# The head and the tail of a conditioned two-layer kernel: earlier weight transfers, one more table pair before the first layer, and GpSimd's store ahead of its power

## The chip, the core and the metric

The kernel runs on one core of a Trainium2 chip. The core has five engines with a queue each: TensorE (PE in the rows, PEld for its weight loads), VectorE (DVE), ScalarE (ACT), GpSimd (POOL) and SyncE (SP), which only issues transfers. ACT and POOL issue transfers too. The metric is the device time of one execution in microseconds; the median of three is quoted. The profile is one further execution; its span runs from the first to the last recorded instruction.

## What is computed

128 sequences of 64 tokens with 256 features go through two layers. The first is chosen for each sequence by `itok_B_0_2` (kind NR, TSR or SR, else nothing is added), the second by one of 16 experts (`itok_B_0_15`). Both end in a residual and a layer norm.

```
out_nr  = gelu(x @ w1_nr + b1_nr) @ w2_nr + b2_nr
out_tsr = gelu(x @ w1_tsr + b1_tsr) @ w2_tsr + b2_tsr
out_sr  = gelu(gelu(x @ w1_sr + b1_sr) @ w2_sr + b2_sr) @ w3_sr + b3_sr
out = where(c == 0, out_nr, where(c == 1, out_tsr, where(c == 2, out_sr, 0)))
x = layernorm(x + out) * gamma + beta
...
hidden = gelu(x @ down_W.T + down_b)
hidden = hidden @ expert_W[idx].T + expert_b[idx]        # if the domain is valid
hidden = (hidden + domain_emb[idx]) @ up_W.T + up_b
return layernorm(hidden + x) * ln_gamma + ln_beta
```

## The kernel before

**Sort.** A head sorts the sequences by kind on the core itself: VectorE makes one-hot columns of the ids, TensorE sums them up, VectorE turns the sums into a place for each sequence. The result is `MOVES`, rows to load and to store (semaphores `s_load_ids`, `s_store_ids`), and `IDS`. From then on the work goes in slots of four sequences of one kind, 256 tokens each; with padding there are 33 slots here, 0 to 32.

**Precision.** Every operand of a large product is split in a high and a low part: ACT copies the high part (`weight_high`, `table_high`, `input_high`), VectorE subtracts it from the full value (`weight_low`, `table_low`, `input_low`), GpSimd does so for the hidden values (`low`). TensorE multiplies high by high, high by low and low by high.

**Tables.** The expert's matrix and the up projection are folded into one table for each expert. `table_pair(j)` makes two of 18 tables on TensorE, `table_high(j)` and `table_low(j)` split them. The pairs use three banks of PSUM in turn (`table_bank`), so from the fourth on (j = 3) a pair waits until the low part of an earlier one is taken. In the kernel before, three pairs (`EARLY_PAIRS`) are made in the head; pairs 3 and 4 come in step -1, 5 and 6 in step 0, 7 and 8 in step 1 (`PAIRS_IN_STEP`).

**Steps.** Every engine runs its own stream of steps, written out by hand in a fixed order: step g holds the layers of slot g and g + 1 and the later stages of slots g - 1 to g - 4. Steps -1 to 3 are unrolled (HEAD); then come a loop of plain steps (MAIN), a loop whose steps look at the number of slots (LATE), and DRAIN, the two steps behind the last slot. In step -1 TensorE runs the first layer of slot 0 (`start_sr`, 24 products), the tables of the step and the residual of slot 0, which waits for `s_store_ids`. In step 0 it runs half of the middle layer (`middle_layer`, with `w2_sr`), then the first half of slot 1's first layer, which waits for `x_lo`, the low part of slot 1's input.

**Queues in the head.** SP issues ids, `w1_sr`, `w1_two`, and once the sort is done two sequences of slot 0 and four of slot 1. ACT issues the first part of `per_unit` and of `per_feature` and the last bias, copies the high part of `w1_sr`, waits for the sort, issues the other two sequences of slot 0 and then `w2_sr`, the rest of `per_unit`, `last` and the rest of `per_feature`. Only then does it take up the tables and the input.

**Stores.** A slot's output goes out in two ways: SP stores one half with plain transfers, GpSimd the other with an indirect one (`store_tile`, 128 rows of 1 KB). VectorE's `finish` writes the output buffer of a slot and waits first for three things: `rstd` (the power that GpSimd computes), and for both stores of the slot before that used this buffer (`st_out`, `sc_out`). There are two buffers, so slot 30 waits for slot 28. In the last LATE step (g = 32) GpSimd computes power 32, then power 33, then stores slot 28. In DRAIN it stores 29 and 30 and computes power 34, then computes power 35 and stores 31 and 32.

The rows of the profile leave out numbers in names: `w_sr_sb` is w1_sr or w2_sr, `w_two` is w1_two, `x` is the input of either parity.

## Time and profile before

| | us |
|---|---|
| median of 3 runs | 293.97 |
| lowest, highest | 293.71, 295.15 |
| profiled execution, own time | 294.8 |
| profiled execution, span | 293.0 |
| TensorE busy in the span | 267.2 |
| VectorE, ScalarE, GpSimd busy | 197.2, 203.5, 149.4 |

The own time of the profiled execution is 1.8 us above its span: what lies around the recorded instructions. It is 0.83 us above the median. TensorE is busy nearly without a gap from 25 us to 258 us; it has idle time in the head, while the sort runs and the first weights and inputs come in, and in the tail, from 263 us on. After 286 us only transfers and the end of the program are left.

### The profile page before, as it was taken

How to read it: one execution, taken by the hardware profiler on the slowest of the kernel's cores; microseconds unless marked ns; L12 is line 12 of the kernel's file. 1: busy time of each engine (PE TensorE's matmuls, PEld its weight loads, DVE VectorE, ACT ScalarE, POOL GpSimd, SP SyncE). 2: the span in 40 equal slices, each digit the busy share in tenths (PEclk: the TensorE clock that was granted, in tenths of full speed). 3: DMA queues.
4: the chain of work that ended last, by engine and by line, in shares of the span. 5: the costliest groups of instructions: out<-in, count | busy, mean ns of one | idle time of the engine just before them, and what ended most of it. 6: DMA issues, size and time to landing. Idle time of an engine off the chain costs nothing.

```text
span 293.0 us, 8411 instructions
## 1 busy us (share of the span) xinstructions
PE 267.2 (91%) x2053; PEld 255.3 (87%) x2054; DVE 197.2 (67%) x669; ACT 203.5 (69%) x451; POOL 149.4 (51%) x164
## 2 busy tenths in 40 slices
PE   6879999999999999899999999999999999998410
PEld 6669999999999998799999999999999999997310
DVE  7486623426744844778888788888788887878360
ACT  3157687867777683887878888878878788776100
POOL 3211724734746654556655566545656455562450
PEclk9997999999999999999999999999999999999955
DMA  6561210110221122123242332423223332311121
GB/s 200 138 198 26 57 36 2 41 39 10 47 72 37 49 59 55 35 72 81 71 111 78 88 81 69 101 81 98 73 70 101 86 99 72 92 38 45 57 66 36
DMA packets 44029, 21.00 MB, mean 72 GB/s; under 512 B 37783, under 2 KB 42182, under 8 KB 44008
## 3 DMA queue, kind: packets, MB, share of 16 engines
q1 hardware_dynamic: 41142, 13.95, 19.7%
q0 software_dynamic: 1584, 4.33, 4.1%
q10 hardware_dynamic: 1282, 2.45, 2.8%
q8 instruction: 11, 0.18, 0.3%
q14 instruction: 10, 0.08, 0.1%
HBM read 12.02 MB, written 8.65 MB: 71 GB/s over the span
## 4 chain that ended last, share of the span: by engine, by line
PE 80%; issue 7%; DMA 4%; DVE 3%; POOL 2%; ACT 1%; ACTq 1%; POOLq 1%; DVEq 0%
PE ps_h L943 18%; PE ps_z L1012 10%; PE ps_u L1058 9%; PE ps_d L1067 9%; PE ps_z L1017 5%; PE ps_z L978 5%; PE ps_t L1029 5%; PE ps_u L978 4%; PE ps_t L1116 3%; PE ps_t L1117 3%; PE ps_z L1000 3%; PE ps_t L1119 3%; DMA w_sr_sb<-in_w_sr 2%; DMA out<-o,out_rows_now 1%; PE ps_u L912 1%
## 5 line engine op out<-in xcount | busy, mean ns | idle before, releaser
L446 POOL TENSOR_TENSOR h_lo<-h,h_hi 128x256 fp32r<-128x256 f32 (+1 forms) x75 | 69.7, 930 | 95.6 <-ACT h L805 95.5
L451 POOL TENSOR_TENSOR rs<-ve,minus_half 128x4 f32<-128x4 f32 x36 | 40.9, 1135 | 26.7 <-DVE ve L642 26.6
L805 ACT ACTIVATE h_hi<-ps_h,per_feature_sb 128x256 fp32r<-128x256 f32 x84 | 38.2, 479 | 20.3 <-PE ps_h L943 20.1
L630 DVE BATCH_NORM_STATS2 st<-ps_z 128x6 f32<-128x256 f32 x66 | 24.8, 414 | 33.1 <-PE ps_z L1017 33.1
L812 ACT ACTIVATE zn<-ps_z,nm,rs 128x256 f32<-128x256 f32 x66 | 33.7, 561 | 9.1 <-DVE nm L646 8.5
L461 POOL DMA_INDIRECT out<-o,out_rows_now x33 | 34.9, 1057 | 9.3 <-issue 6.1
L805 ACT ACTIVATE h<-ps_h,per_feature_sb 128x256 f32<-128x256 f32 x84 | 38.0, 481 | 0.0
L829 ACT ACTIVATE yt<-ps_t,per_feature_sb 128x256 f32<-128x256 f32 x66 | 34.0, 573 | 5.2 <-PE ps_t L1029 5.1
L1058 PE MATMUL ps_u<-table_hi,stack 128*128 x132 | 36.5, 306 | 0.0
L1067 PE MATMUL ps_d<-yt,per_feature_sb 128*128 128x256 f32 x132 | 34.1, 380 | 1.3 <-ACT yt L829 1.3
L1058 PE MATMUL ps_u<-table_lo,stack_hi 66*128 x132 | 33.7, 285 | 0.0
L602 DVE TENSOR_TENSOR x_lo<-x,x_hi 128x512 fp32r<-128x512 f32 x33 | 22.8, 690 | 14.9 <-ACT x_hi L787 14.9
L1012 PE MATMUL ps_z<-last_lo,h_hi 128*128 (+1 forms) x132 | 32.4, 279 | 0.0
L1012 PE MATMUL ps_z<-last_hi,h_hi 128*128 (+1 forms) x132 | 32.4, 279 | 0.0
L691 DVE SCALAR_TENSOR_TENSOR o<-n,rs,per_feature_sb 128x256 f32<-128x256 f32 x66 | 28.8, 477 | 0.0
L666 DVE SCALAR_TENSOR_TENSOR n<-ps_u,mv,per_feature_sb 128x256 f32<-128x256 f32 x66 | 28.2, 465 | 0.1
L943 PE MATMUL ps_h<-x_hi,w_two_lo 128*128 128x256 f32 x96 | 26.9, 280 | 0.0
L943 PE MATMUL ps_h<-x_hi,w_two_hi 128*128 128x256 f32 x96 | 26.9, 280 | 0.0
L943 PE MATMUL ps_h<-x_lo,w_two_hi 128*128 128x256 f32 x96 | 26.9, 280 | 0.0
L653 DVE BATCH_NORM_STATS2 st<-ps_u 128x6 f32<-128x256 f32 x66 | 25.0, 420 | 1.6 <-PE ps_u L1058 1.6
L1012 PEld LDWEIGHTS ps_z<-last_hi,h_hi 128*128 128x128 f32 x132 | 24.8, 188 | 1.1
L1012 PEld LDWEIGHTS ps_z<-last_lo,h_hi 128*128 128x128 f32 x132 | 24.8, 188 | 1.0
(153 smaller groups left out, 694.8 us busy)
## 6 DMA issues: line engine op xcount, KB each, us to landing
x<-in_x_feat SPq DMA_DIRECT2D x130, 64.0 KB
out<-o SPq DMA_DIRECT2D x66, 64.0 KB, 2.0
last_sb<-in_last_w ACTq DMA_DIRECT2D x1, 768.0 KB, 8.7
out<-o,out_rows_now POOLq DMA_INDIRECT x33, 2.7
w_sr_sb<-in_w_sr SPq DMA_DIRECT2D x1, 512.0 KB, 3.5
w_two_sb<-in_w_two SPq DMA_DIRECT2D x1, 512.0 KB, 4.3
w_sr_sb<-in_w_sr ACTq DMA_DIRECT2D x1, 512.0 KB, 6.6
per_unit_sb<-in_per_unit ACTq DMA_DIRECT2D x1, 325.0 KB
```

The lines of the kernel that those rows point to most:

```text
L446: pool.tensor_tensor(dst, full, high.bitcast(F32), ALU.subtract).then_inc(ready, 1)
L451: pool.tensor_tensor(RS[p][:, :, :], VE[p][:, :, :], mhalf[:, :].rearrange("p (n t) -> p n t", n=2), ALU.pow).then_inc(rstd, 1)
L461: pool.indirect_dma_start(out_rows, row, O[p][:, 1, :], None).then_inc(sc_out[p], 16)
L666: ins = dve.scalar_tensor_tensor(out=N2[p][:, t, :], in0=UP[p][:, t, :], scalar=MV[step][:, 1, t, 0:1], in1=G2[:, 0, :], op0=ALU.subtract, ...
L691: dve.scalar_tensor_tensor(out=O[q][:, t, :], in0=N2[q][:, t, :], scalar=RS[p][:, 1, t:t + 1], in1=G2[:, 1, :], op0=ALU.mult, op1=ALU.add) ...
L805: ins = act.activation(dst[:, m, :], src[m], ACT.Gelu, bias=COL[:, bass.ds(col + m, 1)])
L812: ins = act.activation(ZN[:, t, :], ZP[p][:, t, :], ACT.Identity, bias=NM[p][:, t:t + 1], scale=RS[p][:, 0, t:t + 1])
L829: ins = act.activation(YT[q][:, c, :], TP[:, c, :], ACT.Identity, bias=COL[:, COL_BETA1 + c:COL_BETA1 + c + 1], scale=COL[:, COL_G1 + c:CO ...
L943: ins = pe.matmul(out_ap, lhs[a], rhs[b], start=first and n == 0, stop=last and n == 2)
L1012: pe.matmul(ZP[p][:, t, :], h2h[:, c, t * P:(t + 1) * P], rows(half, c), start=False, stop=False)
L1058: ins = pe.matmul(UP[p][:, t, :], flat(stack[:, t, :, :])[:, d * T:d * T + P], table[:, bass.ds(at[2 * t + d], H)], start=False, stop=(tab ...
L1067: ins = pe.matmul(DP[:, 0:N], DD[:, c, :], YT[q][:, c, :], start=(c == 0), stop=(c == KC - 1))
```

## The change

In the head, ACT issues `w2_sr` and the rest of `per_unit` right behind its first two transfers, during the sort. `last` and the rest of `per_feature` go to SP, behind the input of slot 1. ACT warms up its gelu table ahead of all this, and copies the high part of `w1_two` during the sort instead of in step -1. Four table pairs are made in the head instead of three; ACT and VectorE take the first two ahead of the input of slot 0 (one before). The fourth stands on TensorE where six filler products (`keep_busy`) stood. Step -1 keeps pair 4 only. In a LATE step GpSimd stores before it computes the power of the step behind the last.

```diff
-        EARLY_PAIRS = 3
+        EARLY_PAIRS = 4
-        PAIRS_IN_STEP = {-1: (3, 4), 0: (5, 6), 1: (7, 8)}
+        PAIRS_IN_STEP = {-1: (4,), 0: (5, 6), 1: (7, 8)}
...
             load(rows_to_load(1), 1)
+            sp.dma_start(W["last"][:, :], W_DRAM["last"]).then_inc(s_w_in["last"], 16)
+            sp.dma_start(FEAT[:, EARLY_FEAT:], per_feature[:, EARLY_FEAT:]).then_inc(s_norm_in, 16)
...
+                store(g, p, where)
                 if where == LATE:
 
                     with pool.If(g + 1 >= n_slots):
                         power(g + 1, 1 - p)
-                store(g, p, where)
...
-            table_low(0)
+            for j in range(2):
+                table_low(j)
             input_low(0, 0)
...
-            for j in range(1, EARLY_PAIRS):
+            for j in range(2, EARLY_PAIRS):
                 table_low(j)
             weight_low("w2_sr")
...
+            act.wait_ge(s_const, 1)
+            act.activation(gelu_warm[:, :], ones[:, 0:1], ACT.Gelu)
             act.wait_ge(s_ids_in, 16)
             act.dma_start(UNIT[:, 0:EARLY_UNIT], per_unit[:, 0:EARLY_UNIT]).then_inc(s_unit_in, 16)
             act.dma_start(FEAT[:, 0:EARLY_FEAT], per_feature[:, 0:EARLY_FEAT]).then_inc(s_feat_in, 16)
+            act.dma_start(W["w2_sr"][:, :], W_DRAM["w2_sr"]).then_inc(s_w_in["w2_sr"], 16)
+            act.dma_start(UNIT[:, EARLY_UNIT:per_unit.shape[1]], per_unit[:, EARLY_UNIT:]).then_inc(s_unit_rest_in, 16)
...
-            act.wait_ge(s_const, 1)
-            act.activation(gelu_warm[:, :], ones[:, 0:1], ACT.Gelu)
             weight_high("w1_sr")
+            weight_high("w1_two")
...
-            act.dma_start(W["w2_sr"][:, :], W_DRAM["w2_sr"]).then_inc(s_w_in["w2_sr"], 16)
-            act.dma_start(UNIT[:, EARLY_UNIT:per_unit.shape[1]], per_unit[:, EARLY_UNIT:]).then_inc(s_unit_rest_in, 16)
-            act.dma_start(W["last"][:, :], W_DRAM["last"]).then_inc(s_w_in["last"], 16)
-            act.dma_start(FEAT[:, EARLY_FEAT:], per_feature[:, EARLY_FEAT:]).then_inc(s_norm_in, 16)
...
-            table_high(0)
+            for j in range(2):
+                table_high(j)
             input_high(0, 0, 0)
-            for j in range(1, EARLY_PAIRS):
+            for j in range(2, EARLY_PAIRS):
                 table_high(j)
...
-                        if where == HEAD and g < 0:
-                            weight_high("w1_two")
...
             pe.matmul(TP[0:TE, 0, :], BE[:, :], UPB, start=True, stop=True).then_inc(s_const_ps, 1)
+            for j in range(TABLE_BANKS, EARLY_PAIRS):
+                table_pair(j)
 
             pe.wait_ge(s_ids, 1)
-            keep_busy(H0, 6)
```

ACT's queue in the kernel before, from its second sequence of slot 0 to the high part of `w2_sr`:

```order
L332 DMA x0<-in_x_feat 128x2x64
L779 DMA w2_sr_sb<-in_w2_sr 128x1024
L780 DMA per_unit_sb<-in_per_unit 65x1280
L781 DMA last_sb<-in_last_w 128x1536
L782 DMA per_feature_sb<-in_per_feature 128x512
L305 TENSOR_LOAD bounds
L766 CAST table_hi<-ps_u0 128x512
L787 CAST x_hi0<-x0 128x512
L766 CAST table_hi<-ps_u1 128x512
L766 CAST table_hi<-ps_d 128x512
L770 CAST w2_sr_hi<-w2_sr_sb 128x1024
```

The same stretch of ACT's queue in the changed kernel:

```order
L332 DMA x0<-in_x_feat 128x2x64
L305 TENSOR_LOAD bounds
L773 CAST table_hi<-ps_u0 128x512
L773 CAST table_hi<-ps_u1 128x512
L789 CAST x_hi0<-x0 128x512
L773 CAST table_hi<-ps_d 128x512
L773 CAST table_hi<-ps_u1 128x512
L777 CAST w2_sr_hi<-w2_sr_sb 128x1024
```

Four transfers have gone from between the input's issue and the tables, and two tables stand ahead of the input's copy. Two of the four stand at the start of ACT's queue now:

```order
L762 ACTIVATE gelu_warm<-ones 128x1
L764 DMA per_unit_sb<-in_per_unit 65x1056
L765 DMA per_feature_sb<-in_per_feature 128x271
L766 DMA w2_sr_sb<-in_w2_sr 128x1024
L767 DMA per_unit_sb<-in_per_unit 65x1280
L769 DMA last_b_sb<-in_last_b 3x256
L777 CAST w1_sr_hi<-w1_sr_sb 128x1024
L777 CAST w1_two_hi<-w1_two_sb 128x1024
```

All of these run before the sort hands out the rows. GpSimd's queue at the end of a LATE step of odd g, before:

```order
L498 COMPARE_AND_BRANCH
L450 REGISTER_ALU
L451 TENSOR_TENSOR rs0<-ve0,minus_half 128x4
L498 UNCONDITIONAL_BRANCH
L458 REGISTER_ALU
L461 DMA out_0<-o1,out_rows_now1 8960x256
```

and in the changed kernel:

```order
L460 REGISTER_ALU
L463 DMA out_0<-o1,out_rows_now1 8960x256
L501 COMPARE_AND_BRANCH
L452 REGISTER_ALU
L453 TENSOR_TENSOR rs0<-ve0,minus_half 128x4
L501 UNCONDITIONAL_BRANCH
```

The store has moved ahead of the branch and of the power under it; the pieces shown are those of odd g, and those of even g (32 is the last here) read alike with the other buffers.

## Rows read from the trace of the kernel before

**Rows 1.** The page, busy time (share of the span) and instructions of each engine.

```profile
PE 267.2 (91%) x2053; PEld 255.3 (87%) x2054; DVE 197.2 (67%) x669; ACT 203.5 (69%) x451; POOL 149.4 (51%) x164
```

**Rows 2.** The chain of waits in order of time: start, us, what.

```profile
10.41 6.59 DMA w_sr_sb<-in_w_sr
```

**Rows 3.** Timeline of ACT, 7 to 24 us: start, us, instruction, idle before.

```profile
8.96 1.42 ACTq L332 DMA_DIRECT2D x<-in_x_feat  x2
...
12.15 0.44 ACTq L782 DMA_DIRECT2D per_feature_sb<-in_per_feature  x1
13.20 0.59 ACT L766 CAST table_hi<-ps_u 128x512 fp32r<-128x512 f32 x1 [6.76 <-issue]
13.68 0.62 ACT L787 CAST x_hi<-x 128x512 fp32r<-128x512 f32 x1
...
22.04 0.62 ACT L787 CAST x_hi<-x 128x512 fp32r<-128x512 f32 x1 [1.56 <-DMA x<-in_x_feat]
```

**Rows 4.** Timeline of DVE, 14 to 24 us.

```profile
14.42 0.67 DVE L602 TENSOR_TENSOR x_lo<-x,x_hi 128x512 fp32r<-128x512 f32 x1
...
16.40 0.67 DVE L595 TENSOR_TENSOR table_lo<-ps_d,table_hi 64x512 fp32r<-64x512 f32 x1
18.11 1.23 DVE L571 TENSOR_TENSOR w_sr_lo<-w_sr_sb,w_sr_hi 128x1024 fp32r<-128x1024 f32 x1 [1.05 <-ACT w_sr_hi L770]
...
21.41 0.19 DVE L619 CAST moves<-store_row 1x72 int32<-1x72 f32 x1
...
23.32 0.67 DVE L602 TENSOR_TENSOR x_lo<-x,x_hi 128x512 fp32r<-128x512 f32 x1
```

**Rows 5.** Timeline of PE, 8 to 26 us.

```profile
8.64 1.99 PE L912 MATMUL ps_u<-per_unit_sb 64*128 64x256 f32 x8
...
11.96 1.60 PE L901 MATMUL ps_h<-ones 128*128 128x128 f32 x12
...
22.46 0.56 PE L1116 MATMUL ps_t<-h_hi,w_sr_hi 128*128 128x256 f32 x1
...
25.17 0.30 PE L943 MATMUL ps_h<-x_hi,w_sr_hi 128*128 128x256 f32 x1
```

**Rows 6.** PE in two stretches: us, busy (instructions), granted clock, DMA share, GB/s.

```profile
18.38:21.79 3.41, 2.03 (x9) 1.00 0.38 94
21.80:25.20 3.40, 3.40 (x17) 0.50 0.01 2
```

**Rows 7.** Timeline of ACT, 2 to 3.3 us.

```profile
2.57 0.64 ACTq L759 DMA_DIRECT2D per_unit_sb<-in_per_unit  x1
```

**Rows 8.** Queues between 4 and 5 us: packets, MB, share of 16 engines (q1 is SP's).

```profile
q1 hardware_dynamic: 115, 0.41, 99.9%
```

**Rows 9.** The page, issue of w1_two by SP: KB, us to landing (issued at 1.71).

```profile
w_two_sb<-in_w_two SPq DMA_DIRECT2D x1, 512.0 KB, 4.3
```

**Rows 10.** All engines, 9 to 10 us; clock, DMA share and GB/s come last.

```profile
9.00:10.00 1.00, 1.00 (x6) 0.89 (x5) 1.00 (x8) 0.00 (x0) 0.21 (x1) 1.00 0.00 0
```

**Rows 11.** Queues between 12 and 13 us.

```profile
q1 hardware_dynamic: 86, 0.02, 11.1%
```

**Rows 12.** Timeline of POOL, 266 to 273 us.

```profile
266.82 1.04 POOL L451 TENSOR_TENSOR rs<-ve,minus_half 128x4 f32<-128x4 f32 x1 [3.14 <-DVE ve L642]
270.20 1.24 POOL L451 TENSOR_TENSOR rs<-ve,minus_half 128x4 f32<-128x4 f32 x1 [2.33 <-DVE ve L642]
271.62 1.04 POOL L461 DMA_INDIRECT out<-o,out_rows_now  x1 [0.18 <-issue]
```

**Rows 13.** Timeline of DVE, 275 to 281 us.

```profile
275.74 0.15 DVE L689 COPY out_rows_now<-out_rows 128x1 int32 x1 [4.87 <-DMA out<-o,out_rows_now]
...
279.93 0.76 DVE L653 BATCH_NORM_STATS2 st<-ps_u 128x6 f32<-128x256 f32 x2 [0.45 <-PE ps_u L1058]
```

**Rows 14.** Timeline of PE, 273 to 278 us.

```profile
277.30 0.63 PE L978 MATMUL ps_u<-ident,yt 128*128 128x128 f32 x4 [4.07 <-issue]
```

**Rows 15.** TensorE's sequencer, branch of line 1177, 270 to 274 us: ns (min/median/max), start.

```profile
L1177 PEldq COMPARE_BRANCH  x1: 3702/3702/3702, 272.1 to 272.1; - x1
```

More of the change, by code:

```diff
@@ L236, in conditioned_layers @@
         LAST_STEP = S_MAX + 4
-        EARLY_PAIRS = 3
-        EARLY_UNIT = H + 2 * E + 2 * EARLY_PAIRS * 2 * A
+        EARLY_PAIRS = 4
+        TABLE_BANKS = 3
+        EARLY_UNIT = H + 2 * E + 2 * TABLE_BANKS * 2 * A
         EARLY_FEAT = COLS + KC * 2 * A
-        TABLE_BANKS = 3
-        PAIRS_IN_STEP = {-1: (3, 4), 0: (5, 6), 1: (7, 8)}
+        PAIRS_IN_STEP = {-1: (4,), 0: (5, 6), 1: (7, 8)}
         assert TE == 2 * 9
@@ L858, in _ @@
                         gelu(h1[:, 0:2, :], h1h[:, 0:2, :], [H0[:, 0, :], H0[:, 1, :]], COL_B1_SR, h0_hi, h0_full)
-                        if where == HEAD and g < 0:
-                            weight_high("w1_two")
                     with act.Else():
-                        if where == HEAD and g < 0:
-                            weight_high("w1_two")
                         for slot in on_slot(act, g, -1, where, n_slots):
@@ L905, in table_pair @@
                 bank = table_bank(j)
-                if j == EARLY_PAIRS:
+                if j == TABLE_BANKS:
                     pe.wait_ge(s_unit_rest_in, 16)
@@ L930, in _ @@
             pe.wait_ge(s_unit_in, 16)
-            for j in range(EARLY_PAIRS):
+            for j in range(TABLE_BANKS):
                 table_pair(j)
```

## The prediction

> **What bounds the kernel now.** I read the page first: TensorE is busy for 267.2 us of the span [rows 1], and from about 25 us on it works without a gap that matters. So a change pays only where TensorE waits: in the head, and in the tail. The chain of waits in order of time tells for whom. In the head one piece is far longer than the others: the transfer of `w2_sr`, 6.59 us from its issue at 10.41, so landed at 17.00 [rows 2]. ACT issued it only after the inputs of slot 0. Then ACT copies its high part, VectorE starts its low part at 18.11, and behind that on VectorE stand the rows that TensorE needs: `MOVES` at 21.41 (released `s_store_ids`) and the low part of slot 1's input at 23.32 [rows 4]. TensorE takes up slot 0's middle layer at 22.46 and slot 1's first layer at 25.17, the first matmul of the stretch that has no gap [rows 5]. That last time is the one to follow: what it moves, the end moves.
>
> In the tail I read three timelines beside each other. GpSimd starts the store of slot 28 only at 271.62, after power 33 [rows 12]; VectorE stands 4.87 us until it has landed and goes on at 275.74 [rows 13]. TensorE starts slot 32's adapter at 277.30 after 4.07 us that no semaphore explains [rows 14]. Its sequencer tells why: the branch of line 1177, begun at 272.1, took 3702 ns [rows 15].
>
> **The head, step by step.** ACT's last input transfer is issued by 10.38 [rows 3]. Before, 12.15 + 0.44 = 12.59 ended four more issues, and the first table's copy began 0.61 later, at 13.20. Now the same 0.61 (reading the bounds) follows 10.38: first table at 10.99, the second at about 11.5, the input at 12.1 if it has landed. Had it? ACT's two sequences and SP's two were issued from 8.96 on; between 12 and 13 us SP's queue moved only 86 packets [rows 11], the last of slot 0 and the first of slot 1. I take the landing as 12.4; the bounds are 12.1, when ACT is free, and 13.68, when it was used [rows 3].
>
> On ACT then: input 12.4, third table 12.9, fourth table as soon as TensorE has made it. The fourth pair waits on TensorE for VectorE's second low part. That one ends at 10.99 + 0.59 + 2 x 0.62 = 12.8 (VectorE's pace for `table_lo` is 0.6 [rows 4]); a pair costs half of 1.99 [rows 5], so it is made at 13.9. Copy until 14.45, high part of `w2_sr` until 15.5. `w2_sr` has long landed then: issued at about 3.7, behind `per_unit` and `per_feature`.
>
> On VectorE: input low 13.0 to 13.7 (0.67 [rows 4]), the two constants 0.85, third and fourth table 1.2, so free at 15.75. The low part of `w2_sr` starts at 15.76 instead of 18.11: **2.35 us earlier**. Behind it the same instructions follow in the same order up to slot 1's input, so 21.41 becomes 19.06 and 23.32 becomes 20.97. One condition: slot 1's input must be there. Before it was the bound at 22.04, with 1.56 us of waiting [rows 3], because its packets stood behind the 1.8 MB that ACT had issued. Now only its own packets are left; SP issues it as before, from 11.6 on at 0.8 us each, so it lands at about 16, and `last` and the rest of `per_feature` (1 MB, some 2.5 us at the 0.41 MB in a us of [rows 8]) behind it by about 20. Both are in time.
>
> TensorE follows `s_store_ids` at 19.06 and reaches the middle layer at 22.46 - 2.35 = 20.11. Before, this stretch ran at a granted clock of 0.50, the lower level of 1.2 GHz, after a stretch in which it had been busy 2.03 of 3.41 us [rows 6]: 25.17 - 22.46 = 2.71 us, where the full clock would take 1.36. If it does so again, slot 1's first layer starts at 22.82, a gain of 2.35. If the clock is full, the layer starts when its input is ready, 20.97 + 0.67 + 0.1 = 21.74, a gain of 3.43. TensorE has about 1 us less of table work in this stretch, so I expect the low level somewhere; if it comes already during the first layer, where the filler products stood (1.60 us [rows 5]), it is over by the middle layer and costs nothing there. I take **2.7**, nearer to the first case.
>
> What else the head's edits cost. The gelu table ahead of the transfers: they start at 2.57 when the ids are there [rows 7], and the table's load fits ahead of it; nothing to 0.2 us. The filler products gone: their time was idle anyway. The high part of `w1_two`: landed at 1.71 + 4.3 = 6.0 [rows 9], ACT copies it from 6.4 to 7.5 (it copies the equally large `w1_sr` before), free before the sort is done at 8.1; nothing. 837 KB more in the transfers before the sort: the transfer engines moved nothing between 9 and 10 us [rows 10], and at 0.41 MB in a us [rows 8] the 837 KB take 2.0 us from about 7.1 on, so they are through by 9.5, when slot 0's packets start at 10; nothing, at worst 0.5. Two issues more on SP behind slot 1's input: 0.8 us, while SP then waits for VectorE's last-bias rows anyway; nothing.
>
> **Queue order, row against rule.** Would the early transfers slow `w1_two`, which ACT now waits for before it issues inputs? Between 4 and 5 us SP's queue had 99.9% of the engines [rows 8], though ACT's `per_unit` was issued at 2.57 [rows 7]: the later queue waited. The Trainium skill ("DMA: Bandwidth & Descriptors", section "Queues, rings and completion order") says that each transfer engine takes the rows with work in turn, packet by packet. By that rule `w1_two` would share with ACT's transfers, which is the second rival below; the row speaks against it here.
>
> **The tail.** The store of slot 28 moves from 271.62 to behind power 32, which ends at 267.86: about 268.1, done on GpSimd at 269.2, before power 33 at 270.20 is due, so it delays nothing. Landing took 3.98 us from 271.62 (until 275.60); from 268.1 that is 272.1. VectorE would go on at 272.2 instead of 275.74: **3.5 us earlier** on VectorE. What is late next? VectorE writes slot 32's stack and then needs slot 32's `ps_u`. It read it at 279.93, and already then TensorE was the last by 0.45 us [rows 13]. TensorE's start at 277.30 does not come from VectorE but from its own branch, 272.1 + 3.7 = 275.8, plus some reads of registers [rows 14, 15]. The change does not touch that. So of 3.5 us on VectorE nearly all turns into a longer wait for TensorE: **0.1 us** is left (bounds 0 and 0.45), and the last two stores follow as before. The end of the tail gains almost nothing.
>
> **The sum.** 2.7 + 0.1 = 2.8 us. Against the profiled execution: 294.8 - 2.8 = 292.0, span 293.0 - 2.8 = 290.2. The profiled execution is 0.83 above the median of three, so the median becomes 293.97 - 2.8 = 291.2.
>
> **Rivals.**
> First, the tail pays too: if the 4.07 us of TensorE go with VectorE's wait, because what I read as a branch was held up by the same thing (the store landed at 275.60, the branch ended at 275.8), slot 32 comes 3.4 us earlier. Time 291.2 - 3.4 = 287.8. For it: the two ends nearly coincide. Against: the branch has no semaphore, and it began at 272.1, long before. 0.11.
> Second, shared queues: `w1_two` lands at 8 instead of 6.0, ACT copies until 9.1 and issues its two inputs 1 us late; the gain falls to 1.9, time 292.1. 0.09.
> Third, the head's gain is given back: once TensorE runs earlier, slot 2's input, whose issue hangs on VectorE and on SP, comes last in step 1 and eats 1 to 2 us. TensorE's step is then bound by a transfer that had about 1.5 us of room. Time 293.2. 0.10.
> Fourth, slower than before: TensorE, with its filler products gone and 1 us less of table work, falls to the lower clock at about 15 us and stays there. Each stretch like the one of 3.40 us at 0.50 [rows 6] costs 1.7 us of work without gaps. One is in the kernel before; the gain of 2.35 is used up when the low level lasts two such stretches beyond slot 1's first layer, that is past 29 us instead of 25.2. With three: 293.97 - 2.4 + 5.1 - 1.7 = 295.0. For it: the idle time between 17.6 and 19 us is longer than before. Against: from 20 us on TensorE has no gap, and so far 3.4 us of such work brought the full clock back. 0.04.
> That the change does not do what it says is hardly open: the queues in the section on the change show all of it.
>
> **How the numbers follow.** The forecast has 0.66, with 289.6 to 292.4 as its own bounds: gain 1.8 (input landed as late as 13.68) to 3.4, and up to 0.9 from the tail's last matmuls, which ran at 0.50 in part and may not. The range of 8 in 10 takes in the second rival and about half of the third: 289.2 to 293.1. A measurement of this kernel can tell about 0.5%, 1.5 us, from no change: faster means below 292.5. That holds for the forecast nearly whole, for the first rival and most of the second: 0.84. Within: the third, rests of the others: 0.12. Slower: 0.04.
>
> **What would show it.** In the changed trace: ACT's first table at 11.0 and input at 12.4; low part of `w2_sr` at 15.8 on VectorE; slot 1's input not waited for; TensorE's first layer of slot 1 at 21.7 to 22.8. In the tail, relative to the rest: VectorE's wait for the store gone from 4.9 to under 1 us, a wait for `ps_u` of about 3.9 us in its place, and TensorE's branch still at 3.7 us. Wrong would be: a wait of ACT for `w1_two`, a low clock beyond 26 us, a gap of TensorE in step 1, or a branch that got short.

## The result, and the profile after

The changed kernel takes 292.75 us (median of 20 executions, 291.34 to 294.17); the kernel before, beside it, 294.03 us (20 executions, 293.29 to 295.15). The ratio is 0.9954, with a 95% interval of 0.9942 to 0.9965: 1.3 us are gained, where 2.8 were forecast. The direction was right and the time lies in the range (289.2 to 293.1), but the gain is less than half of the one worked out. The profiled execution of the changed kernel took 292.9 us, its span is 291.1; so the two profiles are 1.9 us apart while the medians are 1.3 apart. Both figures are needed further down.

**Head.** ACT, VectorE, GpSimd and TensorE in the changed kernel, timelines from 9 to 25 us (start, us, instruction, idle time before it and its releaser). They answer to [rows 3 to 5].

```profile
9.13 1.39 ACTq L332 DMA_DIRECT2D x<-in_x_feat  x2
10.94 1.07 ACT L773 CAST table_hi<-ps_u 128x512 fp32r<-128x512 f32 x2 [3.45 <-PE ps_u L911]
13.18 0.62 ACT L789 CAST x_hi<-x 128x512 fp32r<-128x512 f32 x1 [1.17 <-DMA x<-in_x_feat]
13.70 0.58 ACT L773 CAST table_hi<-ps_d 128x512 fp32r<-128x512 f32 x1
14.18 0.59 ACT L773 CAST table_hi<-ps_u 128x512 fp32r<-128x512 f32 x1
14.65 1.06 ACT L777 CAST w_sr_hi<-w_sr_sb 128x1024 fp32r<-128x1024 f32 x1
...
19.04 0.64 ACT L789 CAST x_hi<-x 128x512 fp32r<-128x512 f32 x1
```

```profile
16.41 1.20 DVE L573 TENSOR_TENSOR w_sr_lo<-w_sr_sb,w_sr_hi 128x1024 fp32r<-128x1024 f32 x1
...
18.86 0.19 DVE L622 CAST moves<-store_row 1x72 int32<-1x72 f32 x1
...
19.28 1.52 DVE L627 TENSOR_TENSOR last_b_lo<-last_b_sb,last_b_hi 4x256 fp32r<-4x256 f32 x1
20.73 1.21 DVE L573 TENSOR_TENSOR w_two_lo<-w_two_sb,w_two_hi 128x1024 fp32r<-128x1024 f32 x1
21.86 0.68 DVE L604 TENSOR_TENSOR x_lo<-x,x_hi 128x512 fp32r<-128x512 f32 x1
```

```profile
19.25 1.27 POOL L448 TENSOR_TENSOR h_lo<-h,h_hi 128x512 fp32r<-128x512 f32 x1 [9.89 <-ACT h L808]
21.22 2.46 POOL L448 TENSOR_TENSOR h_lo<-h,h_hi 128x512 fp32r<-128x512 f32 x1 [0.70 <-ACT h L808]
```

```profile
14.67 0.55 PE L943 MATMUL ps_h<-x_hi,w_sr_hi 128*128 128x256 f32 x1 [0.59 <-DVE x_lo L604]
...
20.48 0.37 PE L1116 MATMUL ps_t<-h_hi,w_sr_hi 128*128 128x256 f32 x1
...
22.68 0.35 PE L943 MATMUL ps_h<-x_hi,w_sr_hi 128*128 128x256 f32 x1 [0.59 <-DVE x_lo L604]
```

The queue did what the diff says. The first table is copied at 10.94, `w2_sr` is there when ACT gets to it, and slot 1's input is not waited for any more (1.56 us in [rows 3]). But ACT stands 1.17 us for slot 0's input, which lands only at 13.18. TensorE reaches slot 1's first layer at 22.68, 2.49 us ahead of [rows 5], after 0.59 us of waiting for VectorE's `x_lo`.

TensorE in two stretches of the changed kernel (window: length, busy (instructions); behind the other engines the granted clock, the share of the transfer engines and GB/s), against [rows 6]:

```profile
14.22:17.63 3.41, 2.96 (x14) 2.99 (x15) 3.38 (x7) 1.52 (x4) 0.00 (x0) 0.50 0.69 220
17.64:21.05 3.41, 3.41 (x25) 2.88 (x25) 3.24 (x8) 3.41 (x10) 1.27 (x1) 1.00 0.36 136
```

The 1.2 GHz level falls on slot 0's first layer, and the middle layer has its full 2.4 GHz. In the profile of before it was the other way round.

**Tail.** GpSimd, VectorE, TensorE and the branch of TensorE's sequencer (ns min/median/max, start) in the changed kernel, against [rows 12 to 15]:

```profile
264.51 1.04 POOL L453 TENSOR_TENSOR rs<-ve,minus_half 128x4 f32<-128x4 f32 x1 [3.24 <-DVE ve L645]
265.75 1.04 POOL L463 DMA_INDIRECT out<-o,out_rows_now  x1 [0.20 <-issue]
267.90 1.27 POOL L453 TENSOR_TENSOR rs<-ve,minus_half 128x4 f32<-128x4 f32 x1 [1.11 <-DVE ve L645]
```

```profile
269.51 0.15 DVE L692 COPY out_rows_now<-out_rows 128x1 int32 x1 [0.94 <-POOL rs L453]
...
278.04 0.76 DVE L656 BATCH_NORM_STATS2 st<-ps_u 128x6 f32<-128x256 f32 x2 [4.07 <-PE ps_u L1058]
```

```profile
275.20 1.09 PE L978 MATMUL ps_u<-ident,yt 128*128 128x128 f32 x4 [4.28 <-issue]
```

```profile
L1177 PEldq COMPARE_BRANCH  x2: 236/2036/3837, 269.8 to 274.3; - x2
```

The tail reads as forecast. The store of slot 28 stands between power 32 and power 33; VectorE's 4.87 us of waiting for it are 0.94 for a power; in their place VectorE waits 4.07 us for TensorE's `ps_u`; and TensorE's branch still takes 3.8 us.

### The profile page after: what moved, and what is told of

The parts are those of the page before. It is cut to its first block, busy times and chain, and to the rows that moved or that the text cites. A ratio compares the mean times of both kernels' runs of the same rounds, so it can differ in the third digit from the quotient of the medians.

```text
span 291.1 us, 8386 instructions
## 1 busy us (share of the span) xinstructions
PE 267.6 (92%) x2041; PEld 255.4 (88%) x2042; DVE 198.8 (68%) x669; ACT 203.3 (70%) x451; POOL 150.7 (52%) x164
## 4 chain that ended last, share of the span: by engine, by line
PE 80%; issue 8%; DVE 4%; POOL 2%; DMA 1%; ACT 1%; SPq 1%; POOLq 1%; ACTq 0%; DVEq 0%
PE ps_h L943 18%; PE ps_z L1012 10%; PE ps_u L1058 10%; PE ps_d L1067 9%; PE ps_z L1017 5%; PE ps_z L978 5%; PE ps_t L1029 5%; PE ps_u L978 4%; PE ps_z L1000 3%; PE ps_t L1116 2%; PE ps_t L1119 2%; PE ps_t L1117 2%; PE ps_t L900 2%; POOL out L463 2%; PE ps_u L911 1%
## 5 line engine op out<-in xcount | busy, mean ns | idle before, releaser
L448 POOL TENSOR_TENSOR h_lo<-h,h_hi 128x256 fp32r<-128x256 f32 (+1 forms) x75 | 70.9, 945 | 92.2 <-ACT h L808 92.1
L604 DVE TENSOR_TENSOR x_lo<-x,x_hi 128x512 fp32r<-128x512 f32 x33 | 22.8, 691 | 16.1 <-ACT x_hi L789 16.1
L1058 PEld LDWEIGHTS ps_u<-table_lo,stack_hi 66*128 66x128 f32 x132 | 25.6, 194 | 0.0
```

The lines of the kernel that those rows point to most:

```text
L448: pool.tensor_tensor(dst, full, high.bitcast(F32), ALU.subtract).then_inc(ready, 1)
L1058: ins = pe.matmul(UP[p][:, t, :], flat(stack[:, t, :, :])[:, d * T:d * T + P], table[:, bass.ds(at[2 * t + d], H)], start=False, stop=(tab ...
```

## The experiments

There are eleven runs in three groups: nine new kernels, and the kernel before and the changed kernel once more each. The runs of one group ran on the same chip beside the kernel before (medians 294.22, 294.11 and 294.17 there). A landmark is the time, from the start of the span, at which a certain instruction starts in the trace.

### 1. Head alone, tail alone

`h1_head_only` is the changed kernel with GpSimd's old order:

```diff
-                store(g, p, where)
                 if where == LATE:
...
                         power(g + 1, 1 - p)
+                store(g, p, where)
```

> The changed kernel with GpSimd's old order in a LATE step (power ahead of the store); the head is the changed one. My theory A: the whole gain comes from the head, the store's new place is worth 0.1 us at most, so this takes the changed kernel's time, 1.2 to 1.4 us below the kernel before. Rival B: the store's new place is worth about a microsecond and the head only the rest; then this is 0.2 to 0.6 us below the kernel before.

Measured: 292.79 us (291.63 to 293.86), ratio 0.9948, interval 0.9928 to 0.9968.

`h2_tail_only` is the kernel before with the store ahead of the power.

> The kernel before with the store ahead of the power in a LATE step, nothing else. Theory A: 0 to 0.2 us below the kernel before; in the trace VectorE's wait of 4.9 us for the store is gone and a wait of about 4 us for ps_u stands in its place. Rival B: 0.8 us or more below.

Measured: 294.43 us (293.38 to 297.5), ratio 1.0018, interval 0.9992 to 1.0044. VectorE and TensorE in its tail:

```profile
271.10 0.15 DVE L689 COPY out_rows_now<-out_rows 128x1 int32 x1 [0.94 <-POOL rs L451]
...
279.37 0.76 DVE L653 BATCH_NORM_STATS2 st<-ps_u 128x6 f32<-128x256 f32 x2 [3.81 <-PE ps_u L1058]
```

```profile
276.54 1.09 PE L978 MATMUL ps_u<-ident,yt 128*128 128x128 f32 x4 [4.01 <-issue]
```

So the gain comes from the head, and for the store's new place alone no gain is seen (the interval of its ratio still allows 0.2 us). Which of the head's edits brings how much no run separates.

### 2. The branch that hides the tail

`h4_no_branch` is the changed kernel with TensorE's last expert stage run without the other half of the branch:

```diff
                     with pe.If(g < n_slots + 1):
...
-                    with pe.Else():
-                        expert(g - 2, p, where)
+                        expert(g - 1, q, where)
```

> The changed kernel; TensorE runs slot 32's adapter right behind slot 31's, in the same DRAIN step, instead of in the next one behind the branch that took 3.8 us. Theory A (the branch hides the tail's gain): TensorE's wait of 4.3 us ahead of it is gone, VectorE reads slot 32's ps_u about 2 us earlier or more, and the time falls by 2.5 to 3.5 us. Rival E: the 4.3 us are not the branch but something that would be waited for anyway; then the time stays within 0.5 us.

Measured: 290.78 us (290.11 to 291.09), ratio 0.9871, interval 0.9852 to 0.989: 2.0 us below the changed kernel, where 2.5 to 3.5 were expected. VectorE, and the sequencer's branch:

```profile
274.91 0.76 DVE L656 BATCH_NORM_STATS2 st<-ps_u 128x6 f32<-128x256 f32 x2 [0.46 <-issue]
```

```profile
L1177 PEldq COMPARE_BRANCH  x1: 3565/3565/3565, 273.4 to 273.4; - x1
```

The branch is as long as before, but now no work stands behind it, and VectorE's wait of 4.07 us for `ps_u` is gone. Measured from TensorE's transposes of slot 31 (`ps_u<-ident,yt`), VectorE's last statistics come 10.48 us later in the changed kernel and 6.86 here: 3.6 us are won there, but only 2.0 reach the end. Most of the rest goes in the last store. SyncE waits 1.7 us for GpSimd's last store in the changed kernel and 3.0 here. From the start of GpSimd's last store to the end of that wait it is 3.0 to 3.1 us in the kernel before and in the changed kernel. It is 4.3 to 4.4 here and in two of the three later kernels without this branch (`e8_old_tail_no_branch`, `r10_branch_and_two`), and 3.5 in the third (`r11_pad_ahead`). What makes it longer no experiment shows.

The trace also tells what goes on during the branch. The changed kernel's row for the queue that carries instructions, q8 (packets, MB, share of the 16 engines), is missing from 265 to 270 us, and from 270 to 274 it reads:

```profile
q8 instruction: 1, 0.02, 2.3%
```

It is one packet of 16 KB that starts at 270.77, 1.0 us into the branch. In the kernel before and here, too, one such packet starts 1.0 us into the long branch. So the branch probably waits for code; that is read from the order of events, and no experiment moved the code.

`e8_old_tail_no_branch` is the same edit on the kernel before, so with the store behind the power.

> The kernel before with only the branch taken away on TensorE: expert(g - 1) runs at the end of the first drain step in place of the second step's other half, whose first instruction came 3702 ns after the branch. Store and power on GpSimd stand as before. Theory A (in the tail two things end at nearly the same time: TensorE behind its branch, and VectorE behind the store on GpSimd; each hides what the other would give): VectorE waits as before for the store (4.87 us ending at 275.74 in before), then needs 2 to 3 us more up to the last statistics, and time falls by 0 to 0.8 us, 293.2 to 294.2, ratio 0.997 to 1.0, although the same edit gave the changed kernel 2.0 us. Theory B (the branch alone bounds the tail, and the place of store and power is worth nothing): the same 2 us as in the changed kernel, 292.2, ratio 0.993.

Measured: 293.54 us (293.24 to 294.27), ratio 0.998, interval 0.9969 to 0.9992: 0.6 us of gain, as theory A had it. VectorE and TensorE:

```profile
273.00 0.15 DVE L689 COPY out_rows_now<-out_rows 128x1 int32 x1 [3.36 <-DMA out<-o,out_rows_now]
```

```profile
274.83 0.58 PE L1058 MATMUL ps_u<-table_hi,stack 128*128 x1 [2.36 <-DVE stack_hi L701]
```

TensorE is early now and waits 2.36 us for VectorE, which waits 3.36 us for the store. The store's move alone gave 0 and the branch alone 0.6; the branch on top of the store's move gave 2.0. Two waits of nearly the same length end close together, TensorE's for its branch and VectorE's for the store. With the store's wait in place the branch's removal pays little, and with the branch in place the store's move pays nothing.

### 3. More work for TensorE ahead of the first layer

`h3_fill` puts five of the six filler products back, around the fourth table pair:

```diff
+            pe.wait_ge(s_ids, 1)
+            keep_busy(H0, 3)
             for j in range(TABLE_BANKS, EARLY_PAIRS):
                 table_pair(j)
-
-            pe.wait_ge(s_ids, 1)
+            keep_busy(H0, 2)
```

> The changed kernel with five filler products of TensorE around the fourth table pair (three ahead, two behind) in place of the six that were taken away. Theory C: part of the head's gain was lost to the granted clock, which now falls to 0.50 during slot 0's first layer; with the fillers it does not fall there, and the median is 0.4 to 1.0 us below the changed kernel's. Rival D: the low clock in the first layer costs nothing, because TensorE waits for slot 1's input afterwards anyway (0.59 us in the changed trace); then the median is the changed kernel's within 0.2 us.

Measured: 293.3 us (292.73 to 293.91), ratio 0.9963, interval 0.9941 to 0.9984, so 0.5 us more than the head alone on the same chip, if anything. Two stretches of TensorE, columns as above:

```profile
14.50:17.90 3.40, 3.40 (x29) 3.24 (x28) 3.33 (x7) 2.87 (x7) 0.05 (x1) 1.00 0.75 217
...
20.70:24.10 3.40, 3.10 (x15) 2.84 (x14) 3.40 (x4) 0.89 (x2) 0.47 (x1) 0.50 0.01 5
```

The first layer had the full clock, and nothing was won, which speaks against theory C. TensorE then had to wait 1.34 us for `MOVES` and 0.29 for `x_lo`, and in this execution the low level came behind the first of these waits, from 20.7 to 24.1, in the middle layer and slot 1.

### 4. How far apart are two profiles of one kernel?

`e5_before_again` is the kernel before, profiled once more; `r9_after_again` the changed kernel, profiled and timed once more.

> This is the kernel before, unchanged, profiled once more. What it tells: how much of the distance between the two profiles belongs to the one execution that was profiled. In the profile of before TensorE ran at 0.50 of its clock from 21.79 to 25.20 us, in slot 0's middle layer, and came to slot 1's first layer at 25.17; the kernel with only the new tail, whose head is that of before, had its low stretch at 16.51 to 19.92 and came there at 24.27. Theory A (the place of the low stretch differs from execution to execution, and the price of the change has to be read against a spread of about 1 us): low stretch elsewhere than 21.79, slot 1's first layer at 24.2 to 24.5, x0's landing (first x_hi copy) anywhere in 13.6 to 14.4, span 291.9 to 292.6. Theory B (the stretch belongs to the program of before, and the change takes it away): low stretch at 21.8 again, 25.1 to 25.2, span 292.9.

> The changed kernel, unchanged, once more: profiled again and timed beside the two kernels below. Five heads of the changed order gave slot 1's first layer at 22.35 to 23.33 us, four heads of the order before gave 23.72 to 25.17. Theory A (the place of the low stretch of TensorE's clock in slot 0 moves that landmark by about 0.6 us from execution to execution): somewhere in 22.6 to 23.4, time 292.75 within 0.4, ratio 0.9954 within 0.0013. Theory B (the landmark belongs to the program): 22.68 again.

Measured: `e5_before_again` one execution of 294.52 us, span 292.7. `r9_after_again` 293.05 us (292.14 to 293.2), ratio 0.995, interval 0.9931 to 0.9969, with slot 1's first layer at 22.88. ACT and VectorE in `e5_before_again`:

```profile
13.92 0.59 ACT L766 CAST table_hi<-ps_u 128x512 fp32r<-128x512 f32 x1 [7.48 <-issue]
14.40 0.62 ACT L787 CAST x_hi<-x 128x512 fp32r<-128x512 f32 x1
...
15.87 1.07 ACT L770 CAST w_sr_hi<-w_sr_sb 128x1024 fp32r<-128x1024 f32 x1
```

```profile
17.72 1.20 DVE L571 TENSOR_TENSOR w_sr_lo<-w_sr_sb,w_sr_hi 128x1024 fp32r<-128x1024 f32 x1
...
20.58 1.41 DVE L624 TENSOR_TENSOR last_b_lo<-last_b_sb,last_b_hi 4x256 fp32r<-4x256 f32 x1
21.92 1.21 DVE L571 TENSOR_TENSOR w_two_lo<-w_two_sb,w_two_hi 128x1024 fp32r<-128x1024 f32 x1
23.06 0.67 DVE L602 TENSOR_TENSOR x_lo<-x,x_hi 128x512 fp32r<-128x512 f32 x1
```

In this execution nobody waits for `w2_sr`: it is there at 15.87, when ACT gets to it, and not at 17.00 as in [rows 2]. Nor does VectorE wait for its high part: the low part follows at 17.72 straight behind a table. `h2_tail_only` and `e8_old_tail_no_branch` read alike on VectorE. What is late in all three is slot 0's input: ACT's issues of the four other transfers end at 13.0 to 13.1 instead of 12.59, the first table's copy follows 0.8 us behind, and the input's copy comes at 14.3 to 14.4 without a wait for the landing. So in three of four executions of the old head `w2_sr`'s transfer did not hold the chain; the time that ACT spent on the issues did.

The landmarks of all executions whose head is that of before or of the changed kernel:

| profile | head | `x_hi` slot 0 | `w2_sr` low part | `x_lo` slot 1 | slot 1's first layer | clock at 0.50 in the head |
|---|---|---|---|---|---|---|
| before | old | 13.68 | 18.11 | 23.32 | 25.17 | 21.8 to 25.2 |
| h2_tail_only | old | 14.38 | 17.71 | 23.11 | 24.27 | 16.5 to 19.9 |
| e5_before_again | old | 14.40 | 17.72 | 23.06 | 24.26 | 16.1 to 19.5 |
| e8_old_tail_no_branch | old | 14.30 | 17.62 | 22.90 | 23.71 | none |
| after | new | 13.18 | 16.41 | 21.86 | 22.68 | 14.2 to 17.6 |
| r9_after_again | new | 13.37 | 16.61 | 22.06 | 22.88 | 14.6 to 18.0 |
| h1_head_only | new | 12.96 | 16.20 | 22.45 | 23.27 | none |
| h4_no_branch | new | 13.15 | 16.39 | 21.84 | 23.24 | 13.8 to 20.6 |

The mean of slot 1's first layer is 24.35 for the old head and 23.02 for the new one: 1.3 us, like the medians. With four executions each that spread by 1.5 and 0.6 us, so close an agreement is in part luck. The profile that the prediction rested on is the latest of the four by 0.9 us. Without it the three others give 24.08 against 23.02, 1.1 us. So the low stretch belongs to the execution: theory A for the kernel before (its span, 292.7, came out 0.1 above what I had given it). For the changed kernel the second profile differs from the first by 0.2 us only and tells the theories apart poorly. Two profiles of the kernel before differ in this landmark by more than half of what the change is worth.

The tails of the profiles differ as well. From slot 31's transposes to VectorE's last statistics it is 10.07 us in before and 10.48 in `e5_before_again`, 10.48 and 10.44 in the two profiles of the changed kernel, and 9.28 in `h3_fill`, which has the same tail. TensorE's granted clock falls to 0.50 at 273.6 us in the changed kernel's profile, ahead of slot 32, and at 276.7 in `h3_fill`'s. The sequencer's branch takes 3.44 us in `h3_fill` and 3.58 to 3.86 in the other executions of this code. That is why the two first profiles are 2.49 us apart at slot 1's first layer and 1.9 at the end: 0.2 goes between the head and slot 31's transposes, 0.4 in the tail.

### 5. Who holds slot 1's input on VectorE

In all these kernels GpSimd's `h_lo` of slot 0 runs once or twice between the low part of `w2_sr` and slot 1's `x_lo`, and one or two of VectorE's instructions there take 0.8 to 1.1 us longer than elsewhere. VectorE and GpSimd in `h1_head_only`, where it is two:

```profile
17.98 1.23 DVE L620 TENSOR_TENSOR pad_scratch<-pad_scratch 1x144 f32<-1x144 f32 x1
...
20.00 1.39 DVE L627 TENSOR_TENSOR last_b_lo<-last_b_sb,last_b_hi 4x256 fp32r<-4x256 f32 x1
```

```profile
17.79 1.27 POOL L448 TENSOR_TENSOR h_lo<-h,h_hi 128x512 fp32r<-128x512 f32 x1 [8.43 <-ACT h L808]
19.76 1.35 POOL L448 TENSOR_TENSOR h_lo<-h,h_hi 128x512 fp32r<-128x512 f32 x1 [0.70 <-ACT h L808]
```

`pad_scratch<-pad_scratch` takes 0.30 in the changed kernel's profile and 1.23 here; both long ones end 0.15 to 0.3 us behind GpSimd's instruction. It is 1.9 us of VectorE's time on the way to `x_lo`; TensorE waits for `x_lo` at the end of it:

```profile
23.27 0.36 PE L943 MATMUL ps_h<-x_hi,w_sr_hi 128*128 128x256 f32 x1 [1.28 <-DVE x_lo L604]
```

`e6_two_early` is the changed kernel with one instruction moved out of that stretch:

```diff
+            weight_low("w1_two")
             for j in range(2):
                 table_low(j)
             input_low(0, 0)
...
                 if where == HEAD and g == -1:
-                    weight_low("w1_two")
                     input_low(1, 1)
```

> The changed kernel with one VectorE instruction moved: the low half of w1_two (1.21 us at 20.73, directly ahead of slot 1's x_lo) is computed ahead of the first table_lo, in a gap of 0.94 us at 10.6 where VectorE waits; its operand is there from 7.5. Theory A (the head's gain was cut because slot 1's x_lo is held by VectorE, on which GpSimd's h_lo stretches two instructions by about 1 us): slot 1's x_lo at 20.7 instead of 21.86 (at 21.3 where the first layer has full clock, 22.45 in the run with the old tail); TensorE then goes from slot 0's middle layer into slot 1's first layer without its wait of 0.59 to 1.28 us, at 22.1; the first table_lo 0.2 us later, paid by nobody. Time 292.1, between 0.6 and 1.2 less than the changed kernel's 292.75, ratio to before 0.991 to 0.9935. Theory B (what is gained in step 0 is given back in step 1, where other work waits): the same landmarks, but time 292.6 to 292.9, ratio 0.995. Theory C (x0's landing, taken at 12.4 and measured at 13.18, is the whole of the missing gain and VectorE's order no part of it): slot 1's first layer does not move.

Measured: 291.86 us (291.43 to 292.17), ratio 0.9923, interval 0.991 to 0.9935, so 0.9 us below the changed kernel's 292.75. The two long instructions are there again (`pad_scratch` 1.23, `last_b_lo` 1.39), but `x_lo` comes at 21.53 (21.3 was expected at the full clock) and TensorE goes on at 22.35 without a wait. Theory A holds: VectorE's queue between `w2_sr` and `x_lo` was the bound of the new head where the low level of the clock is short or absent. Earlier by 0.9 than in `h1_head_only`, whose clock in the head is the same, the landmark is passed on to the end in full.

`e7_bias_behind` moves the split of the last bias behind slot 1's `x_lo`.

> The changed kernel with the split of the last layer's bias (two VectorE instructions, 0.27 and 0.41 us alone, the second stretched to 1.52 beside GpSimd's h_lo) moved behind slot 1's x_lo. It asks what the stretching hits. Theory A (whatever VectorE runs while GpSimd's h_lo of 1.27 us runs ends after it): w1_two's low half, 1.2 us alone, stands there instead and takes 1.8 to 2.4; x_lo of slot 1 at 21.0 to 21.5 instead of 21.86, so 0.3 to 0.8 us are won for TensorE's slot 1. Theory B (only short instructions of few partitions are stretched, a full one shares): w1_two's low half keeps 1.2 and x_lo comes at 20.2. Against both stands SyncE, which waits for this bias ahead of its loads for slot 2: they go out at about 27 instead of 24.94, and if slot 2's x is then late for its x_hi copy the time does not fall. Time 292.3 if the loads have the room, 293 or more if they don't; ratio to before 0.993 or 0.997.

Measured: 293.12 us (292.07 to 293.96), ratio 0.9968, interval 0.9955 to 0.998, so no gain over the changed kernel and perhaps a loss of 0.4. VectorE and GpSimd:

```profile
18.84 1.21 DVE L573 TENSOR_TENSOR w_two_lo<-w_two_sb,w_two_hi 128x1024 fp32r<-128x1024 f32 x1
19.98 1.75 DVE L604 TENSOR_TENSOR x_lo<-x,x_hi 128x512 fp32r<-128x512 f32 x1
```

```profile
19.22 1.96 POOL L448 TENSOR_TENSOR h_lo<-h,h_hi 128x512 fp32r<-128x512 f32 x1 [9.85 <-ACT h L807]
```

Theory B had the start of `x_lo` (20.2 forecast) but not its length; theory A had neither. VectorE's `w_two_lo`, which was under way when GpSimd's instruction started, kept its 1.21; GpSimd's took 1.96 instead of 1.27; and the next of VectorE, `x_lo`, took 1.75 instead of 0.67. The one that has begun finishes, and the other waits. They do not take turns strictly: in the changed kernel GpSimd's second `h_lo`, begun at 21.22 under `w_two_lo`, took 2.46 us, while `x_lo` went ahead of it with its 0.68. `x_lo` starts 1.9 us earlier than in the changed kernel but ends only 0.8 earlier.

Why did the time not fall? Two things lie near. SyncE's loads for slot 2 went out at 27.50 instead of 24.94, as the expectation feared, and ACT waited for slot 2's input, which it copies at 30.09 without a wait in the changed kernel:

```profile
32.01 0.62 ACT L788 CAST x_hi<-x 128x512 fp32r<-128x512 f32 x1 [1.66 <-DMA x<-in_x_feat]
```

That cost TensorE nothing that can be seen: from slot 1's first layer to slot 31's transposes it is 244.87 us here and 244.88 in the changed kernel. The other is the clock, at 0.50 from 13.4 to 20.2 us in the profiled execution. There TensorE does not wait for `x_lo`; it works without a gap from its first layer on and reaches slot 1's at 23.01, where 22.68 was the changed kernel's. So in this execution the low clock took what the new order gave. Whether it does so in the others, no run tells: the profiled execution took 292.33 us, 0.8 less than the median.

### 6. The best of it

`r10_branch_and_two` is the changed kernel without the branch and with `w1_two`'s low half early.

> The changed kernel with both edits that gained by themselves: TensorE's drain without the branch (2.0 us), and w1_two's low half ahead of the first table_lo (0.9 us). Theory A (head and tail are two ends of one chain that meets in the loop's period, and add): 289.9, ratio 0.985 to 0.987, with 0.984 at best. Theory B (they overlap: what the head brings is taken by VectorE's own end in the tail once the branch is gone): 290.6 to 290.8, ratio 0.9885 to 0.989.

Measured: 289.95 us (289.1 to 291.32), ratio 0.9871, interval 0.9844 to 0.9898. The sum of the two gains (2.0 and 0.9) from 292.75 would be 289.85; the time lies there, though the ratio's interval, wide as it is, does not exclude the smaller gain of theory B. Two of the six executions took 291.3 us, and the mean is 290.2.

`r11_pad_ahead` puts the five instructions that end in `MOVES` ahead of `w2_sr`'s low half as well:

```diff
-            weight_low("w2_sr")
-
             dve.wait_ge(s_pad, 1)
...
+            weight_low("w2_sr")
```

> The kernel of the run before this one, with the five small VectorE instructions that make the rows to store (pad_scratch, store_row, MOVES) put ahead of w2_sr's low half, in place of behind it. TensorE waited 1.34 us for MOVES ahead of slot 0's transposes, because MOVES read the PSUM bank that they write and GpSimd's h_lo had stretched one of the five from 0.30 to 1.23 us. Theory A (the stretch hits whoever meets h_lo on VectorE, and here the five end at 17.9, before h_lo begins at 18.0): five instructions at 16.4 to 17.9 with 0.3 us each, w2_sr's low half at 17.9 to 19.1, slot 0's middle layer begins at 19.3 to 20.0 instead of 20.55, slot 1's x_lo at 20.6 to 21.5, slot 1's first layer at 21.2 to 21.8 instead of 22.35; time 0.5 to 1.0 less than the run before, 289.0 to 289.4. Theory B (w2_sr's low half becomes the last thing that the middle layer waits for, or the low stretch of the clock falls in): middle layer at 20.5 or later, time the same within 0.3.

Measured: 289.71 us (288.52 to 290.05), ratio 0.9847, interval 0.9823 to 0.9871. VectorE and GpSimd:

```profile
17.08 0.29 DVE L619 TENSOR_TENSOR pad_scratch<-pad_scratch 1x144 f32<-1x144 f32 x1
...
17.86 1.21 DVE L573 TENSOR_TENSOR w_sr_lo<-w_sr_sb,w_sr_hi 128x1024 fp32r<-128x1024 f32 x1
```

```profile
19.09 1.31 POOL L448 TENSOR_TENSOR h_lo<-h,h_hi 128x512 fp32r<-128x512 f32 x1 [9.73 <-ACT h L807]
```

TensorE begins slot 0's middle layer at 20.16 and slot 1's first layer at 21.62 (20.57 and 22.03 in `r10_branch_and_two`). The low stretch from 13.6 to 17 us kept GpSimd away from the five instructions in any case, so this execution does not test that part of theory A. Against `r10_branch_and_two` the median is 0.2 us lower, less than the intervals can tell. It is the fastest kernel that ran, 4.5 us or 1.5% below the kernel before.

## Where the prediction was right and where it failed

**The landmark: right.** Slot 1's first layer is what moves the end. From it to slot 31's transposes it is 244.7 to 245.0 us in old and new heads alike (the transposes start at 269.86 before and at 267.56 after); only `h3_fill` has 245.2. So at most 0.3 us is given back in between, and the third rival did not come.

**The bound: right for one execution only.** The prediction named `w2_sr`'s transfer, issued behind the inputs of slot 0. In the profile of before it held VectorE by 1.05 us. In the three other executions of the old head it held nobody on VectorE, and ACT's issues ahead of slot 0's input did (section 4). The change moves both, so the direction came out right all the same. In those three the input's copy goes from 14.3 to 14.4 down to 13.0 to 13.4 in the new heads, 1.2 us in the mean, and the low part of `w2_sr` from 17.7 to 16.4 with it.

**The tail's 0.1 us: right as far as it can be told.** `h2_tail_only` shows no gain, the branch of TensorE stayed at 3.8 us when the store moved, and `h4_no_branch` shows that it was what hid the rest. The first rival fell.

**The side costs: right for the most part.** ACT copied `w1_two`'s high part after a wait of 0.45 us, at the time that was forecast; the second rival did not come. The fourth rival, a lower clock that stays, came in part in two of nine profiles of new heads: `h4_no_branch` has 0.50 from 13.8 to 20.6 and `e7_bias_behind` from 13.4 to 20.2, twice as long as in any old head. TensorE reaches slot 1 at 23.24 and 23.01 there, without a wait for VectorE.

**The step that failed: "the low part of `w2_sr` starts at 15.76 instead of 18.11: 2.35 us earlier".** It was mis-sized at both ends.
The new end: slot 0's input was taken to land at 12.4, from bounds of 12.1 and 13.68. In the nine profiles of new heads ACT took it up between 12.96 and 13.37, and it waited 1.17 us for the landing in the changed kernel. I chose a value near the lower bound, when the queue row pointed the other way: between 12 and 13 us SP's queue was still moving the small packets of slot 0 [rows 11]. That shifts the low part to 16.4 and takes 0.65 us.
The old end: 18.11 holds for the one execution in which VectorE waited 1.05 us for ACT's high part, and ACT for the transfer's 6.59 us [rows 2, 4]. In three other executions of the old head it is 17.6 to 17.7. That takes 0.4 us.
2.35 - 0.65 - 0.4 = 1.3 us, the measured gain of the medians. The rest of the 2.8 is the 0.35 for the clock and the 0.1 for the tail.
The lower bound of the gain was wrong as well: 1.8 was given for an input that lands as late as 13.68. That is 1.3 us behind the 12.4, and by the prediction's own steps it leaves 1.4 of the 2.7.

**The step about the clock.** "I take 2.7" added 0.35 us to this for the case in which TensorE escapes the lower clock. The profile of before had that level in slot 0's middle layer, where it costs: 2.71 us [rows 5] instead of 1.5 to 2.0 in the other old heads. It was no property of the kernel: the other old heads have it in the first layer or not at all. And where the new head escapes it altogether (`h1_head_only`), slot 1's first layer comes at 23.27, later than with the low level in slot 0 (22.68).

**"Behind it the same instructions follow in the same order": they do, but not at the same distance.** From the low part of `w2_sr` to slot 1's `x_lo` it is 5.2 to 5.4 us in old heads, 5.45 in new ones with the low level early, and 6.25 in `h1_head_only`. With the input of slot 1 no longer late, ACT runs the gelus of slot 0 without a pause, GpSimd's second `h_lo` comes ahead of `x_lo`, and in `h1_head_only` VectorE is held twice. The forecast of 21.74 at the full clock misses this; it is why the filler products brought nothing, and why `e6_two_early` did.
The Trainium skill ("SBUF — State Buffer", section "Who interferes with whom") states the mechanism: a VectorE instruction with both inputs in SBUF and a GpSimd one that reads SBUF exclude each other, whoever comes first holds the port for the whole instruction, and a VectorE instruction with at most one input in SBUF does not contend outside its two-port modes. The traces agree, with 1.23 us for `pad_scratch<-pad_scratch` beside `h_lo`, and with its neighbour that reads `ps_z` in the kernel before:

```profile
19.58 0.30 DVE L616 TENSOR_TENSOR pad_scratch<-ps_z,pad_scratch 1x144 f32<-1x144 f32 x1
```

`h_lo` starts 0.05 us behind it, and both keep their time (0.30 and 1.26). I had not weighed it against [rows 4].

**The sum was made against the wrong base.** The gain was read as a difference to one execution that lies 0.8 us above the median, and then taken off the median. What made that execution slow (the late `w2_sr`, the clock in the middle layer) was counted as something that the change removes from every execution.

**The landmark's number was luck.** 22.82 was forecast and 22.68 measured, but by another path. The forecast has the middle layer start at 20.11 and run at the lower level for 2.71 us. In the changed kernel it starts at 20.48, runs at the full level, and TensorE then waits 0.59 us for `x_lo`. For the full level the prediction had 21.74, and that is missed by 0.94 us: 0.65 from the later start of `w2_sr`'s low part, and the rest mostly from the longer way to `x_lo` (5.45 instead of 5.21).

## What to carry over

Before a gain is taken as the distance between a planned time and one profiled execution, subtract what is peculiar to that execution: a landing or a stretch of low clock that sits on the critical chain and that makes it slower than the median does not come off the median. When a transfer on the chain is moved forward, what was second is next: here the instructions of VectorE between two landmarks, and moving one of them into a gap gave 0.9 us, two thirds of what the whole change gave. Where two waits end within a microsecond of each other, cost the pair as well as each one: the store's move was worth nothing and the branch 0.6 us, together they were worth 2.0. And before a wait on the chain is called the bound, see in a second execution whether it is there.

## What the runs showed of the hardware

- VectorE and GpSimd hold each other up over operands in SBUF, also for tiny ones: a 1x144 subtraction of 0.30 us took 1.14 to 1.27 us beside a 128x512 one on GpSimd, and a GpSimd instruction of 1.27 us took 1.96 when VectorE was first (`e7_bias_behind`), 2.46 when two of VectorE went ahead (the changed kernel). A cast of 1x72 that reads SBUF, `moves<-store_row`, took 1.24 instead of 0.19 in `h2_tail_only`.
- The branch of line 1177 on TensorE's sequencer took 0.07, 3.70 and 0.23 us in its three executions in the tail of the kernel before, and 3.30 to 3.86 us the second time in the other profiles. In `h4_no_branch`, whose other half is empty, the third took 2.83. During the long one a packet of 16 KB is moved on the instruction queue. Moving the work behind it ahead of it was worth 2.0 us.
- TensorE's granted clock fell to 0.50 at different places in the head in executions of the same program (16.1 to 19.5 and 21.8 to 25.2 us for the kernel before), always after a stretch in which TensorE had been idle for part of the time. Such idle time does not always bring it: `e5_before_again` and `e8_old_tail_no_branch` have the same head and the same 2.24 us of idle time ahead of the first layer, and the second has the full clock throughout the head. Slot 1's first layer moved by up to 1.5 us among the old heads.
